# Layer 0 attention: masking every fourth head after the exponential on GpSimd instead of with identity products on TensorE

## The reference, cut to what matters

```python
scores = jnp.einsum('bhqd,bhkd->bhqk', Q, K) / scale        # 16 x 16 x 256 x 256
scores = jnp.where(mask, scores, NEG_INF)                   # NEG_INF = -1e10; mask is (batch, 1, query, key)
attention = jax.nn.softmax(scores, axis=-1)
heads_out = jnp.einsum('bhqk,bhkd->bhqd', attention, V)
x = x + jnp.tanh(g_xattn[0]) * (heads_out @ W_proj.T + b_proj)
```

## Time and profile before

| | |
|---|---|
| median of 3 runs | 1293.08 us (1290.47 to 1293.56) |
| the profiled execution | 1296.06 us, span 1294.8 us |
| granted TensorE clock over the span | 0.984 |
| TensorE busy | 94% of the span |
| VectorE busy | 69% |
| ScalarE busy | 55% |
| GpSimd busy | 37% |

### The profile page before, as it was taken

One profiled execution on the slowest core, in us unless ns is written; L12 is line 12 of the kernel. 1 busy time (PEld: TensorE's weight loads), 2 busy tenths in 40 slices (PEclk: granted clock), 3 DMA queues, 4 the chain that ended last, 5 costly groups with the idle time before them and its releaser, 6 DMA issues.

```text
span 1294.8 us, 25126 instructions
## 1 busy us (share of the span) xinstructions
PE 1212.6 (94%) x9236; PEld 858.0 (66%) x9236; DVE 894.7 (69%) x2680; ACT 710.4 (55%) x1197; POOL 480.4 (37%) x675
## 2 busy tenths in 40 slices
PE   6799999999999989999999989999999999888998
PEld 5466667666776664444448866676676776577987
DVE  2678767886777646589999956767868777642333
ACT  1355555555655548889983326666566665622221
POOL 5344333443343100057000434343643643322555
PEclk8899999999999999999999999999999999988999
DMA  5422334233432032000003644364464342137983
GB/s 158 140 79 82 109 92 128 80 87 107 121 104 67 11 97 84 1 1 1 1 1 124 198 138 116 99 161 136 135 170 123 117 137 61 51 144 230 312 198 39
DMA packets 121941, 137.22 MB, mean 106 GB/s; under 512 B 12881, under 2 KB 116427, under 8 KB 121797
## 3 DMA queue, kind: packets, MB, share of 16 engines
q1 hardware_dynamic: 111888, 125.98, 32.9%
q0 software_dynamic: 7296, 8.15, 3.5%
q10 hardware_dynamic: 2634, 1.49, 0.4%
HBM read 58.42 MB, written 27.36 MB: 66 GB/s over the span
## 4 chain that ended last, share of the span: by engine, by line
PE 56%; DVE 6%; issue 3%; ACT 2%; DMA 1%; POOL 1%; SPq 1%; ACTq 0%; POOLq 0%; DVEq 0%
PE PS L641 14%; PE PS L687 5%; PE PS L444 5%; PE PS L384 5%; PE PS L427 4%; PE PS L655 4%; PE PS L403 4%; PE PS L502 2%; PE PS L696 2%; PE PS L476 2%; PE PS L391 2%; DVE NM L1086 1%; PE PS L520 1%; PE PS L485 1%; ACT P L808 1%
## 5 line engine op out<-in xcount | busy, mean ns | idle before, releaser
L808 ACT ACTIVATE P<-PS 128x512 f32<-128x512 f32 x512 | 302.2, 601 | 165.0 <-PE PS L430 98.3
L1083 DVE CUSTOM_DVE_ANT_0 MX<-PS,NQ 128x256 bf16<-128x256 f32 x512 | 192.5, 418 | 66.9 <-PE PS L403 66.6
L427 PE MATMUL PS<-QS,KS 99*128 99x256 bf16 x1024 | 225.7, 274 | 8.1 <-ACT P L808 7.1
L1086 DVE TENSOR_REDUCE NM<-PS 128x2 f32<-128x512 f32 x256 | 173.6, 685 | 75.9 <-PE PS L403 71.4
L403 PE MATMUL PS<-KS,QS 96*128 96x256 bf16 x1024 | 196.8, 275 | 23.4 <-DVE NM L1083 15.1
L403 PEld LDWEIGHTS PS<-KS,QS 96*128 96x128 bf16 x1024 | 87.0, 98 | 89.0 <-DVE NM L1083 28.2
L444 PE MATMUL PS<-P,V 128*32 128x256 f32 x2048 | 137.0, 385 | 1.5 <-ACT P L808 1.5
L427 PEld LDWEIGHTS PS<-QS,KS 99*128 99x128 bf16 x1024 | 95.2, 99 | 53.9 <-ACT P L808 20.5
L430 PE MATMUL PS<-NK,identb 128*128 128x256 bf16 x512 | 126.9, 273 | 0.0
L641 PE MATMUL PS<-XNT,wup 128*128 128x512 f16 x576 | 124.9, 379 | 0.0
L641 PEld LDWEIGHTS PS<-XNT,wup 128*128 128x128 f16 x576 | 56.2, 98 | 67.4
(11 more groups left out here) (233 smaller groups left out, 2476.1 us busy)
## 6 DMA issues: line engine op xcount, KB each, us to landing
KS<-PP SPq DMA_DIRECT2D x192, 128.0 KB, 2.9
QS<-PP SPq DMA_DIRECT2D x192, 128.0 KB, 2.4
WH<-in_wex SPq DMA_DIRECT2D x16, 768.0 KB
WG<-in_wex SPq DMA_DIRECT2D x10, 768.0 KB
bufd<-bias_row SPq DMA_DIRECT2D x5, 1032.0 KB, 12.2
XB<-in_x SPq DMA_DIRECT2D x16, 256.0 KB, 2.9
CT<-in_ctxT SPq DMA_DIRECT2D x16, 256.0 KB, 3.1
x1d<-XB SPq DMA_DIRECT2D x16, 256.0 KB, 2.1
```

The lines of the kernel that those rows point to most:

```text
L427: ins = tensor.matmul(o, t.KS[b % 3][0:99, h, 128 * kt:128 * kt + 128], t.QS[b % 3][0:99, h, :], start=True, stop=(L == 1))
L808: scalar.activation(t.P[h % 8][:, :, :], PS[:, h % 2, :].rearrange("p (k n) -> p k n", k=2), ACT.Exp).then_inc(s_ex, 1)
L1083: ins = vector.tensor_tensor_reduce(t.MX[:, 2 * (h % 2) + qt, :], PS[:, bk, 256 * qt:256 * qt + 256], t.NQ[b % 4][:, qt, :], -1.0, 1.0e30, ...
L1086: ins = vector.tensor_reduce(nm[:, :, h], PS[:, bk, :].rearrange("p (t n) -> p t n", t=2), X, ALU.max, negate=True)
```

## The change

For heads 0, 4, 8 and 12 of layer 0 the two identity products go, and the bank holds the score less the masked maximum. After the exponential, GpSimd takes the smaller of it and one (for a key that doesn't count, the exponential may be larger than one) and multiplies it with `MK`, a table of ones and zeros, both in place in `P`. The group's product with V waits for that (`s_pm`). A query without any key that counts needs a row of ones in `MK`: TensorE sums `NK` over the keys with two products with a matrix of ones (`pe_marks`), VectorE compares the sum with a bound and takes the larger of the result and the mask (`dve_marks`). The mask of batch s+3 may be loaded once `MK` of batch s+1 is made. To make room, `w_r` moves into `AM`, and six semaphores are merged into others.

```diff
+def masked_after(L, h):
+    return L == 0 and h % 4 == 0
+
+def mark_at(s, k):
+    if (s, k) == (-2, 6):
+        return 0
+    return s + 2 if k == 14 and 1 <= s + 2 < NB else None
...
         def pe_scores_t(L, b, h):
-            pe.wait_ge(d_i, 48 * (L + 1))
+            pe.wait_ge(d_i, 16 + 48 * (L + 1))
...
-                if L == 0:
+                on_scores = L == 0 and not masked_after(L, h)
...
+                if on_scores:
                     ins = tensor.matmul(o, identb[:, :], t.NK[b % 4][:, kt, :], start=False, stop=True)
...
         def pe_av(L, b, g):
             pe.wait_ge(s_ex, 16 * n + 4 * g + 4)
+            if L == 0:
+                pe.wait_ge(s_pm, 4 * b + g + 1)
...
+        def pe_marks(b):
+            bk = odd_bank(("mk", b), s_mk, b + 1)
+            pe.wait_ge(s_cst, 1)
+            pe.wait_ge(s_pen, b + 1)
+            for kt in range(2):
+                ins = tensor.matmul(PS[:, bk, 0:256], onesb[:, :], t0.NK[b % 4][:, kt, :], start=(kt == 0), stop=(kt == 1))
+            ins.then_inc(s_mc, 1)
...
+        def dve_marks(b):
+            dve.wait_ge(s_mc, b + 1)
+            dve.wait_ge(s_pm, 4 * (b - 2))
+            vector.scalar_tensor_tensor(t0.MK[b % 3][:, :, :], bc(PS[:, home["mk", b], 0:256], 1, 2), (S - 0.5) * NEG,
+                                        t0.MM[b % 2][:, 2:4, :], ALU.is_le, ALU.max).then_inc(s_mk, 1)
...
         def dve_slot(L, s, k):
+            if L == 0 and (s, k) == (-2, 8):
+                dve_marks(0)
+            if L == 0 and k == 0 and 1 <= s + 1 < NB:
+                dve_marks(s + 1)
...
+        def pool_mask(b, h):
+            pool.wait_ge(s_mk, b + 1)
+            pool.wait_ge(s_ex, 16 * b + h + 1)
+            p = t0.P[h % 8][:, :, :]
+            gpsimd.tensor_scalar(p, p, 1.0, None, ALU.min).then_inc(*pool.tick())
+            pool.wait_ge(*pool.last())
+            gpsimd.tensor_tensor(p, p, t0.MK[b % 3][:, :, :], ALU.mult).then_inc(s_pm, 1)
...
         def pool_slot(L, s, k):
+            if L == 0 and 0 <= s < NB and k in (1, 7, 9, 13):
+                pool_mask(s, {1: 0, 7: 4, 9: 8, 13: 12}[k])
...
         def sp_load_mask(b):
+            sp.wait_ge(s_mk, b - 1)
```

More of the change, by code:

```diff
@@ L217, in late_tiles @@
                 t.NK = [tile(m, f"NK{i}", [128, 2, 256], BF16) for i in range(4)]
+                t.MK = [tile(m, f"MK{i}", [128, 2, 256], BF16) for i in range(3)]
         top0 = ExitStack()
@@ L235, in build @@
         w_s = tile(m, "w_s", [128, 48], F32)
-        w_r = tile(m, "w_r", [128, 48], F32)
+        w_r = AM[:, 48:96]
         m.close()
@@ L304, in build @@
         TL = (t0, t1)
-        s_cst, s_g, s_tg, s_tgb, s_cr, d_cr = (sem(n) for n in ("s_cst", "d_g", "s_tg", "s_tgb", "s_cr", "d_cr"))
+        s_cst, s_g, s_tg, s_tgb, s_cr = (sem(n) for n in ("s_cst", "d_g", "s_tg", "s_tgb", "s_cr"))
         d_x = [sem(f"d_x{i}") for i in range(5)]
@@ L314, in build @@
         d_i, s_iv = sem("d_i"), sem("s_iv")
+        s_mc, s_mk, s_pm = (sem(n) for n in ("s_mc", "s_mk", "s_pm"))
         s_av, s_pen, s_var, s_rs, s_xn, s_xb = (sem(n) for n in ("s_av", "s_pen", "s_var", "s_rs", "s_xn", "s_xb"))
@@ L326, in build @@
         s_gd, s_gp = sem("s_gd"), sem("s_gp")
-        s_z, d_z = sem("s_z"), sem("d_z")
+        d_z = sem("d_z")
         s_xq, s_xh, s_xl, s_ff, s_fa, s_fm, s_uq, s_vq = (sem(n) for n in (
@@ L333, in build @@
         d_we = [sem(f"d_we{i}") for i in range(4)]
-        d_wr, s_num, s_bs, d_base = (sem(n) for n in ("d_wr", "s_num", "s_bs", "d_base"))
+        s_bs, d_base = (sem(n) for n in ("s_bs", "d_base"))
         s_rm, s_lg, s_sub, s_rex, s_oh, s_cn, s_pos, s_sl = (sem(n) for n in (
@@ L418, in pe_scores_t @@
             i = 16 * n + h
-            pe.wait_ge(d_i, 48 * (L + 1))
+            pe.wait_ge(d_i, 16 + 48 * (L + 1))
             pe.wait_ge(d_n[h // 8][b % 3], 16 * uses(L, b, 3))
             pe.wait_ge(s_ex, i - 1)
-            if L == 0:
+            if L == 0 and not masked_after(L, h):
                 pe.wait_ge(s_pen, n + 1)
@@ L426, in pe_scores_t @@
                 o = PS[:, bk, 256 * kt:256 * kt + 256]
+                on_scores = L == 0 and not masked_after(L, h)
                 ins = tensor.matmul(o, t.KS[b % 3][0:99, h, 128 * kt:128 * kt + 128], t.QS[b % 3][0:99, h, :],
-                                    start=True, stop=(L == 1))
-                if L == 0:
+                                    start=True, stop=not on_scores)
+                if on_scores:
                     ins = tensor.matmul(o, identb[:, :], t.NK[b % 4][:, kt, :], start=False, stop=True)
@@ L515, in pe_router @@
             bk = odd_bank(("lg", b), s_lg, b + 1)
-            pe.wait_ge(d_wr, 16)
+            pe.wait_ge(d_ql, 64)
             pe.wait_ge(s_xmt, NB + b + 1)
@@ L579, in pe_slot @@
                     pe_ranks(GROUP_OF[s - 2][0])
+            if L == 0 and mark_at(s, k) is not None:
+                pe_marks(mark_at(s, k))
             if L == 0 and wq_step(s, k) in range(3 * WQ):
@@ L794, in act_setup @@
             act.wait_ge(s_cr, 1)
-            scalar.dma_start(crd, XNf[0:3, 0:2048]).then_inc(d_cr, 16)
+            scalar.dma_start(crd, XNf[0:3, 0:2048]).then_inc(d_i, 16)
         def act_ones(L):
-            act.wait_ge(d_cr, 16)
+            act.wait_ge(d_i, 16)
             for i in range(3):
@@ L850, in act_values @@
             n, t = L * NB + b, TL[L]
-            act.wait_ge(s_iv, 3 * L + min(b, 2) + 1)
+            act.wait_ge(s_iv, min(b, 2) + 1 if L == 0 else (5, 7, 8)[min(b, 2)])
             act.wait_ge(s_ah, 4 * (n - 2))
@@ L1230, in dve_route_rows @@
             vector.tensor_scalar(xms[:, :, D + 1], sm, tg[:, 3:4], None, ALU.mult)
-            dve.wait_ge(s_num, 1)
+            dve.wait_ge(s_iv, 6)
             vector.tensor_copy(xms[:, :, D], NUM[:, 2 * b0:2 * b0 + w])
@@ L1586, in pool_masks @@
             pool.wait_ge(s_st, 16 * (b - 3))
+            pool.wait_ge(s_mc, b - 3)
             gpsimd.tensor_scalar(t.NK[b % 4][:, :, :], t.MM[b % 2][:, 2:4, :], -1.0, -NEG, ALU.add, ALU.mult).then_inc(s_pen, 1)
@@ L1700, in pool_program @@
                         pool_values(0, i)
-            gpsimd.memset(bias_row[:, :, :].rearrange("p i n -> p (i n)")[:, 0:D + 2], 0.0).then_inc(s_z, 1)
+            gpsimd.memset(bias_row[:, :, :].rearrange("p i n -> p (i n)")[:, 0:D + 2], 0.0).then_inc(s_iv, 1)
             pool_gate_int(0)
@@ L1716, in pool_program @@
             gpsimd.iota(NUM[:, :], pattern=[[128, 32]], base=1, channel_multiplier=1,
-                        allow_small_or_imprecise_dtypes=True).then_inc(s_num, 1)
+                        allow_small_or_imprecise_dtypes=True).then_inc(s_iv, 1)
             for s, k in late_slots():
@@ L1851, in sp_program @@
                 sp_slot(0, s, k)
-            sp.wait_ge(s_z, 1)
+            sp.wait_ge(s_iv, 4)
             zero_row = bias_row[:, :, :].rearrange("p i n -> p (i n)")[:, 0:D + 2]
@@ L1867, in sp_program @@
                     sp_slot(1, s, k)
-            sync.dma_start(WR[:, :, :], a["wr"].rearrange("(k p) n -> p k n", p=128)).then_inc(d_wr, 16)
+            sync.dma_start(WR[:, :, :], a["wr"].rearrange("(k p) n -> p k n", p=128)).then_inc(d_ql, 16)
             for s, k in late_slots():
```

## The result

The changed kernel takes 1328.85 us, median of 4 runs (1325.58 to 1331.36); the kernel before, run beside it on the same chip, 1293.32 us (1290.47 to 1295.31). The ratio is 1.0275, 95% interval 1.0244 to 1.0306: 35.5 us slower. I had forecast 1294 and a range of 1286 to 1301.

The account below looks back on a forecast made before the run. TensorE, the fullest engine, was taken to bound slots 10 to 5, waiting for VectorE in slots 5 to 9. Savings -7.7, head 4's delay +8.5 and +0.2 gave +1.0 us: 1294 us on the median, range 1286 to 1301.

Parts of the forecast that it names:

- GpSimd's pair: Smaller-of-one and mask product on GpSimd: 2.03 us from GpSimd free to the product with V begun, ends 1.83 and 2.43.
- The mechanism: Head 4's mask, queued behind GpSimd's tables, delays the second product with V by 1.35 us; 8.5 us over 13 batches.
- absorbs and carries: Of head 4's 1.35 us delay, TensorE's spare time takes 0.56; 0.79 goes on until the next slot 5.
- no wait in batches 13 to 15: Batches without tables: no delay at the second product with V, only savings, 2.0 us together.
- the identity products' worth: Two products fewer on TensorE save 0.22 us a head at heads 0, 4 and 12, 0.66 a batch; head 8 nothing.
- a loss for the marks: Two TensorE products in slot 14 cost 0.22 us a batch; VectorE's instruction is hidden and costs nothing.
- TensorE's regime: From slot 10 to the next batch's slot 5 TensorE runs unbroken and VectorE waits, 4.6 us a batch; removed products count there.
- my third rival: Identity products were free because something else holds TensorE; only the 8.7 us of cost stay, 1301.8 us; chance 0.05.
- VectorE blocked by GpSimd: GpSimd's masks lengthen VectorE's XN and XM norms; counted 0, as a rival +6.5 us, 1300.6 us, chance 0.2.
- the cover of XN's place: In slots 9 and 10 TensorE needs head 10's maxima only some 0.9 us after they end, hiding a longer norm.

Follow-up runs that it names:

- e5: The changed kernel with GpSimd multiplying by 1.0 and adding 0.0 in place of the smaller-of-one, so no clamp; 1305.59 us, one run.
- e12: The changed kernel without masking for heads 0, 4, 8 and 12 (no identity products, nothing on GpSimd), marks kept; 1291.68 us, 0.9998 of the kernel before.
- e9: e1 plus a wait: GpSimd begins head 12's mask only once both halves of the XM norm are made; 1301.17 us, 1.0049 of the kernel before.
- e8: The kernel before, identity products in place, plus GpSimd's two operations in the same slots on own buffers nobody waits for; 1309.09 us, 1.0124.
- e1: The changed kernel without the smaller-of-one on GpSimd, the product with the mask kept; 1307.83 us, 1.0108 of the kernel before.
- e11: The changed kernel masking heads 1, 2 and 4 instead, GpSimd's products in slots 2, 3 and 7, no smaller-of-one; 1290.78 us, 0.9984 of the kernel before.
- e2: The whole change with GpSimd's mask of head 4 moved from slot 7 to slot 5, ahead of the tables; 1311.01 us, 1.0127 of the kernel before.

## Why the prediction was wrong

**The step that failed first: the price of GpSimd's pair.** I took the smaller-of-one at 0.62 us with 0.90 as its end, from rows that multiply and add. It measured 1.49. The difference between the change and e5, where the operation does take 0.62, is 23.7 us of the 35.5. I had written that each 0.1 us costs 1.2 us in all, which makes 10 us of 0.87. Of the rest most is the clock, of which I had no term: e5 has two low stretches where the change has nine, and seven of 3.4 us at half the clock are at most 12 us. That GpSimd's other jobs, late by the same amount, make up what is left is likely and not measured by itself. Even my high end for the pair, 2.43 us, was passed by the 2.74 measured.

**The mechanism was right.** The wait stands where I put it, at the second product with V, behind the tables; the distance was worked out to 0.15 us for the price that I assumed (2.03 against 1.88 in e5). It absorbs and carries as described. I also forecast no wait in batches 13 to 15; in the trace after, each has one for GpSimd, 0.8 us ahead of the second product with V in batch 13, 1.4 and 1.9 us ahead of the fourth in 14 and 15.

**The second step: the identity products' worth.** I counted heads 0, 4 and 12 and a loss for the marks, 7.7 us net. The run with just that, e12, is at 0.9998: nothing in the total, and in its trace 0.24 us a batch in the mean where I had 0.44. In a typical batch only head 4 counts. I took unbroken starts for TensorE's regime from slot 10 to slot 5, though I had myself found VectorE's idle time nearly all in slots 0 to 5 and at 13. What was removed at head 0 turned into a wait for VectorE's maxima, and what was removed at head 12 into a wait for ScalarE's exponential. In that my third rival, the products free, was three quarters right.

**The third: VectorE blocked by GpSimd counted at 0.** It costs some 7.6 us at XM alone (e9). I had named XM and set it to nothing, with the cover of XN's place, though the scores of head 0 wait for the maxima right behind it. For XN the cover was there, as the typical batch of e9 shows. With GpSimd's load alone e8 lost 16 us, where I had given this rival 6.5; part of the 16 are GpSimd's own late jobs. (The prediction calls this rival the third in one place; it is the second, and its 6.5 us come from a norm longer by 0.7, not from a whole instruction. And 0.53 for the smaller-of is a seventh less than 0.62, not a fifth. Neither changes the forecast.)
The Trainium skill (SBUF — State Buffer, "Who interferes with whom") has the second to come fully blocked for the whole instruction. By that rule XM lasts as long as GpSimd's product and a little more, and the trace of e1 agrees: 1.24 us beside 1.16. Beside the smaller-of it does not: there the norm took 0.68 to 0.70 us under an instruction of 1.49.

**The sum, redone.** Forecast +1; identity products and marks worth nothing, +7.4; GpSimd's pair at the forecast price costs 12.1 and not 8.7, the blocking included, +3.4; the smaller-of at 1.49 instead of 0.62, with the clock, +23.7: 35.5 (the total of e5 from one run, so two or three us may lie in another term). How much of the 23.7 is the clock is not settled closer than between the 8.6 us of the filling run, in which the filling itself cost time in some batches, and the 12 above.

## What to carry to other kernels

Price an operation by a row of the same operation, not of the same shape: where no such row exists, its end should be a multiple, not half as much again. Before counting removed work as gained, look whether the engine that feeds the next instruction idles there too; the same eight products were worth 2.7 or 9.2 us by the head they belonged to. And an engine with 60% idle time is no free place: ask what it stands in front of in its own queue, and which instruction of its neighbour starts at the same moment.

## What the runs showed of the hardware

GpSimd's smaller-of with a constant, f32 in place on 128x512, takes 1.49 us, and 1.95 with an addition; multiply-and-add on the same data takes 0.62, the product with a bf16 table 1.16. In the changed kernel TensorE paused 1.4 to 2.6 us ahead of the second product with V in twelve of thirteen batches, and in eight of these the granted clock was at its lower level for 3.4 us; filled with dummy products, at none of them. It is no sharp line: the clock fell at shorter pauses too (0.72 us in batch 9 of e5, 1.00 in batch 8 of e9 and e11), and not at one of 1.98 us (batch 1 of the changed kernel). A VectorE tensor_scalar that starts while a GpSimd product runs ends some 0.15 us after the product: it took 1.24 us instead of 0.41 when it started 0.07 us in (e1), and 0.76 when it started 0.55 us in (e8). Under a smaller-of of 1.49 us it ended some 0.76 us after the start of that (0.70 us long from 0.06 us in, 0.50 from 0.26 us in), and one that started 0.5 us in or later kept its 0.41 (e2 and the changed kernel).
